# A graph and mixture block on one core: VectorE takes the moments of a later block ahead of the value's bias

## The reference, cut to what matters

```python
def _layernorm(x, axis=-1, eps=1e-05):
    m = jnp.mean(x, axis=axis, keepdims=True)
    v = jnp.var(x, axis=axis, keepdims=True)
    return (x - m) / jnp.sqrt(v + eps)
...
    enh = node_features + 0.1 * query_emb[None, :]
    Q = (enh @ Wq + bq).reshape(N, H, D)
    K = (enh @ Wk + bk).reshape(N, H, D)
    V = (enh @ Wv + bv).reshape(N, H, D)
...
    xn = _layernorm(x, axis=-1)
    x = x + _L0_gnn_ref(xn, edge_index, edge_type_64, ...) + _L0_mix_ref(xn[None], ...)[0]
```

## Time and profile before

| | |
|---|---|
| median of 3 runs | 2975.46 us (2974.98 to 2976.96) |
| profiled execution, its own time | 2994.86 us |
| its span | 2993.0 us |
| busy: TensorE, VectorE, GpSimd, ScalarE | 75%, 64%, 49%, 29% |
| `stage_project` in the span | about 19.6 to 211 us |

### The profile page before, as it was taken

One profiled execution on the slowest core, in us unless ns is written; L12 is line 12 of the kernel. 1 busy time (PEld: TensorE's weight loads), 2 busy tenths in 40 slices (PEclk: granted clock), 3 DMA queues, 4 the chain that ended last, 5 costly groups with the idle time before them and its releaser, 6 DMA issues. The chain is left out here.

```text
span 2993.0 us, 48887 instructions
## 1 busy us (share of the span) xinstructions
PE 2231.8 (75%) x11266; PEld 1389.1 (46%) x11267; DVE 1922.4 (64%) x3248; ACT 868.0 (29%) x2658; POOL 1478.5 (49%) x1460
## 2 busy tenths in 40 slices
PE   6863667666766766766676748999985999967997
PEld 3431333333333333333333436666654666546886
DVE  5653666666666666666666879999995666541111
ACT  2430011011101101100100177777761555531221
POOL 3555555555555555555555226666644434214442
PEclk9995777777777777777777779999997999978999
DMA  4545878787888788878778837777744444354541
GB/s 151 183 156 172 275 257 266 256 270 247 261 270 265 246 264 265 257 249 272 249 253 265 191 129 233 236 235 237 239 150 149 159 146 169 113 192 182 174 169 55
DMA packets 347414, 636.52 MB, mean 213 GB/s; under 512 B 36018, under 2 KB 224950, under 8 KB 347227
## 3 DMA queue, kind: packets, MB, share of 16 engines
q1 hardware_dynamic: 269259, 373.23, 37.9%
q0 software_dynamic: 77824, 262.55, 27.8%
q10 hardware_dynamic: 272, 0.00, 0.0%
HBM read 461.16 MB, written 175.42 MB: 213 GB/s over the span
## 5 line engine op out<-in xcount | busy, mean ns | idle before, releaser
L698 POOL DMA_INDIRECT s_kv<-kv_d,s_index x832 | 795.0, 956 | 657.6 <-issue 325.0
L829 PE MATMUL s_q_ps<-q,s_is_dst 128*128 x2496 | 511.7, 321 | 399.7 <-DVE s_key L752 272.5
L829 PEld LDWEIGHTS s_q_ps<-q,s_is_dst 128*128 128x128 bf16 x2496 | 210.6, 105 | 572.3 <-issue 506.5
L1190 PE MATMUL a_sum_ps<-a_w,a_is_dst 128*128 128x260 f32 x1664 | 421.8, 397 | 48.4 <-DVE odd_sums L1157 31.5
L748 DVE TENSOR_TENSOR s_key<-s_kv,s_rel_ps 128x1024 f32<-128x1024 f32 x208 | 252.4, 1214 | 230.1 <-remote 222.8
L1125 POOL TENSOR_TENSOR a_w<-a_v,a_w 128x512 f32<-128x512 f32 x208 | 284.7, 1369 | 225.2 <-ACT a_w L1095 173.0
L1190 PEld LDWEIGHTS a_sum_ps<-a_w,a_is_dst 128*128 128x128 f32 x1664 | 300.8, 190 | 169.3 <-DVE odd_sums L1157 123.2
L1103 ACT ACTIVATE a_w<-a_v,a_w 128x64 f32<-128x64 f32 x1248 | 319.9, 334 | 3.9 <-DMA a_v<-v_d 3.8
L834 PE MATMUL s_rel_ps<-rel,s_is_kind 64*128 64x64 bf16 x2496 | 244.7, 207 | 52.5 <-issue 51.9
L647 ACT COPY scores<-s_part 128x32 f32 (+1 forms) x104 | 22.6, 218 | 835.9 <-issue 708.6
L757 DVE TENSOR_REDUCE s_part<-s_key 128x16 f32<-128x1024 f32 x208 | 253.7, 1220 | 10.7
(11 more groups left out here) (295 smaller groups left out, 3030.4 us busy)
## 6 DMA issues: line engine op xcount, KB each, us to landing
v_d<-s_kv SPq DMA_DIRECT2D x208, 512.0 KB
a_v<-v_d SPq DMA_DIRECT2D x208, 512.0 KB, 5.3
s_local<-local_d SPq DMA_DIRECT2D x106, 256.0 KB
xh_d<-h_hid SPq DMA_DIRECT2D x24, 1024.0 KB, 6.9
s_kind<-type_d SPq DMA_DIRECT2D x212, 64.0 KB
s_kv<-kv_d,s_index POOLq DMA_INDIRECT x832
kv_d<-pkv SPq DMA_DIRECT2D x50, 256.0 KB, 2.0
wd<-in_L_ffn_Wd SPq DMA_DIRECT2D x8, 1024.0 KB, 12.2
```

Source lines behind the costliest of these rows:

```text
L698: nc.gpsimd.indirect_dma_start(out=kv[:, g * GROUP + b, :], out_offset=None, in_=R["kv"], in_offset=bass.IndirectOffsetOnAxis(ap=index[:, ...
L829: nc.tensor.matmul(q_ps[b][:, u, :], is_dst[:, h, e], M["q3"][:, bass.ds(regs[g % GROUPS * GROUP + u], 1), j, :] .rearrange("p a c -> p (a ...
L1190: ins = nc.tensor.matmul(sum_ps[g % 2 * GROUP + u][:], is_dst[:, g % WRING, u, :], w[:, g % WRING, u, :], start=True, stop=True)
```

## The change

VectorE's addition of the value's bias becomes a function `add_value`, and `normalise` can call it between the aggregation (L262) and the reciprocal (L265). In the loop it is called there, so the order on VectorE becomes: query, key, the three waits, statistics and aggregation of block g + 2, value of block g, reciprocal, normalised block g + 2. The two calls of `normalise` ahead of the loop stay without it. No instruction is added or taken away, and no other engine's program is changed.

```diff
+            def add_value(u, n):
+                dve.wait_ge(S["v_done"], n + 1)
+
+                dve.wait_ge(S["k_read"], n + 1)
+                nc.vector.tensor_tensor(kv[:, u, C:], v_ps[:], bias[:, 2 * C:], ALU.add).then_inc(S["kv_ready"], 1)
+
+            def normalise(st, w, n, value=None):
...
                 nc.vector.bn_aggr(mv[:], stats[:]).then_inc(S["mv_ready"], 1)
+                if value is not None:
+                    add_value(w, value)
 
                 dve.wait_ge(S["std_ready"], n + 1)
                 nc.vector.reciprocal(rstd[:], std[:]).then_inc(S["rstd_ready"], 1)
...
-                    dve.wait_ge(S["v_done"], g + 1)
-
-                    dve.wait_ge(S["k_read"], g + 1)
-                    nc.vector.tensor_tensor(kv[:, u, C:], v_ps[:], bias[:, 2 * C:], ALU.add).then_inc(S["kv_ready"], 1)
-
                     dve.wait_ge(x_in[u], (i + 2) * 16)
                     dve.wait_ge(S["turned"], g + 1)
                     dve.wait_ge(xn_out[u], (i + 1) * 16)
-                    normalise(st, u, g + 2)
+                    normalise(st, u, g + 2, g)
```

More of the change, by code:

```diff
@@ L253, in _ @@
             nc.vector.memset(zero[:], 0.0).then_inc(S["zeroed"], 1)
-            def normalise(st, w, n):
+            def add_value(u, n):
[3 more added lines that the diff above has]
+            def normalise(st, w, n, value=None):
                 dve.wait_ge(S["xn_ready"], n)
```

## The result

The changed kernel takes 3029.41 us in the median of 4 runs (3026.59 to 3032.63), the kernel before 2976.21 us (2974.98 to 2980.85) beside it: 53 us more, a ratio of 1.0177 with a 95% interval of 1.0164 to 1.019.

What follows compares the result with a forecast made beforehand. The prediction took a sync-queue and VectorE chain closed every block as the bound: 0.74 + 0.54 + 2.04 + 0.53 + 0.18 + 0.64 = 4.67 us. 51.0 us over 49 steps plus 1.24 gave 3028 us, range 3012 to 3051.

Steps and rivals of the forecast that it cites:

- The mechanism: In `stage_project`, sync queue and VectorE close a chain every block instead of every two: 4.67 us against 3.63; chance 0.82.
- store to load: In the sync queue, from the store of key and value to the load of x: 0.91 or 0.57, mean 0.74 us.
- store to statistics: From the normalised block's store being issued to VectorE's statistics starting: 2.04 us, with a median landing of 2.0.
- aggregation to bias: On VectorE, from aggregation to the value's bias: 0.18 us, taken between a lower bound of 0.10 and an upper of 0.28.
- The head and the tail: At `stage_project`'s ends: first bias unmoved at 30.4, a late next store adding 1.24 us, last store equally far behind its bias.
- The wait's total: VectorE's statistics waiting every block for the normalised block's store: 85 to 100 us in all instead of 7.1.
- What the change buys: On VectorE, the bias fills the 0.36 us deviation wait and the 0.52 us value wait goes; both worth nothing.
- The rival on the other side: The change pays: with a store landed within 0.57 us, TensorE sets 3.2 us a block, 2954 us; chance 0.04.
- The clock: Rival: TensorE, busy 65%, falls to a lower clock in `stage_project`; 3094 us or part of it; chance 0.07.
- The DMA's price: Landing time of the stage's DMAs: median kept; the shortest, 1.8 us, would give 4.43 us a block and 3016.
- The part absorbed: Rival: the sync queue gets ahead somewhere, so half the loss remains, 3001 us; chance 0.05.
- no change: Rival: waits for value and store trade places in `stage_project`, pace stays 3.63 us, total 2975 us; chance 0.02.

Runs made afterwards that it cites:

- run 1: Kernel before with only the value's bias moved behind the wait for the normalised block's store, still ahead of the statistics: 3007.02 us against 2988.91, ratio 1.0054.
- run 2: Changed kernel with VectorE's wait for the normalised block's store moved right ahead of the instruction writing that buffer: 3020.21 us against 2988.91 for the kernel before.
- run 5: Changed kernel plus one 128 x 256 VectorE addition a block behind the key, in the time spent waiting for the store: 2655.67 us, ratio 1.0201 to the kernel before.
- run 6: Changed kernel plus one 128 x 256 VectorE addition a block between the aggregation and the value's bias: 2670.47 us, ratio 1.0261 to the kernel before.
- run 3: Changed kernel with the store of key and value issued from ScalarE's queue: 2964.69 us, ratio 0.9918 to the kernel before.
- run 7: Changed kernel with the store of key and value put behind the next block's load and normalised-block store in the sync queue: 2577.56 us, ratio 0.9904 to kernel before.
- run 10: Repeat, in the last group, of the changed kernel with key and value stored behind the next block's load and normalised-block store: 2577.60 us, ratio 0.9899 to kernel before.
- run 8: The changed kernel again, unaltered, on another chip: 2654.85 us, ratio 1.0201 to the kernel before.

## Why the prediction was right

**The mechanism** held: the statistics wait for `xn_d` in every block, the pace is set by the chain of queue and VectorE, and runs 1, 2, 5 and 6 each move the pace by what they move in this chain, run 1 within 0.04 us. Runs 3 and 7 cut it without touching VectorE's order, and the loss goes.

**The terms** of the sum, by the timeline of the changed kernel: store to load 0.74 (foreseen 0.74) and load to store 0.54 (0.54), as means over all blocks; store to statistics 2.13 over 49 blocks (2.04), between 1.93 and 3.03; statistics to aggregation 0.53 (0.53); aggregation to bias 0.10 (0.18), the lower of the two bounds; bias to the issue of its store 0.63 (0.64). Unrounded, the sum is 4.68 where 4.67 was foreseen, by two errors of 0.09 and 0.08 that offset each other. Over 49 steps they would have made 4 us either way.

**The head and the tail.** The loop from the first to the last bias takes 229.3 us, against 177.7 before: 51.6 us more; foreseen were 51.0 + 1.24. The first step is 5.42 us instead of the foreseen 5.9. The first bias, which was to stay at 30.4, came at 29.4; this 1.0 us lies between the 51.6 and the 50.7 of the stage's row. In the traces of the other runs it starts at 29.3 to 30.6, so nothing is read into it.

**The regularity** was wrong: steps of 4.50 and 4.84 in turn were foreseen, and the timeline shows 4.61 and 4.72 in the mean of 24 steps each. The queue's shorter turn is followed by the longer way from the store to the statistics: behind 0.58 us 2.27 (153.15 to 155.42), behind 0.91 us 2.03 (158.14 to 160.17), and 2.23 and 2.00 in the mean over all blocks but the first ones. The mean isn't affected, and why the landing answers to it isn't shown.

**The wait's total** was foreseen at 85 to 100 us and is 108.3. The single wait is 2.21 us in the mean of 49, from 2.08 to 2.43, in the upper part of the foreseen 1.7 to 2.3 and in eight blocks above it; and 49 waits of 1.7 to 2.3 would make 83 to 113 us, so the total was also given too narrowly. In every second block the query and the key end 1.08 us behind the issue of the store of key and value (152.04 to 153.12), in the others after the foreseen 1.3. This has no part in the pace.

**What the change buys.** That it was worth nothing while VectorE waits for the store was right. The rival on the other side priced it, without that wait, at 21 us less than the kernel before. Runs 3, 7 and 10 found 24 to 27 us less, at a pace of 3.07 to 3.08 instead of 3.2. Its condition was made true by another way, a queue in which nothing urgent waits for the bias, and not by a faster landing.

**The clock** didn't fall. TensorE is busy for 147.00 of 226 us, 65%, and the granted clock is 1.00 throughout; the rival drew its case from the scores stage, with the same share and 0.74. It was nearer than that looks: with 0.3 us more idle time a block it fell in run 6. That a fallen clock here and there would fit into the block, as the prediction argued, run 6 bears out; up to 10 us had been allowed for it in the range, and nothing was lost. **The DMA's price**: the Trainium skill's sentence in "DMA: Bandwidth & Descriptors", "Latency and other measured facts", that lighter load makes the fixed cost smaller, agrees in direction only. From 100 to 125 the stage moves 136 GB/s instead of 174, and the median landing of the store is 1.9 us instead of 2.0; the time from its issue to the statistics was no shorter for it, 2.13 in the mean against 1.94 and 2.04.

**The part absorbed** and **no change** are out by the pace in every block.

## What to carry to other kernels

Before an instruction is moved behind a wait, ask what its own signal releases, and follow the queue that it releases to the end: if the thing waited for stands in it further down, in program order, the wait feeds itself, and the latency of a DMA is paid in every round. A small wait for a DMA that shows up every second block, like the 7.1 us here, is the sign that such a chain is already near. An order that loses for this reason may be a good one: putting the slow member of the queue behind the urgent ones made a gain of 1% out of a loss of 1.8%.

## What the runs showed of the hardware that was not expected

The mean busy share doesn't tell TensorE's clock. In the changed kernel it is busy for 65% of 226 us, in bursts of 3 us with idle stretches of 1.65 in the mean and at most 2.1, and stays at the upper of its two levels. In the scores stage of the kernel before it is busy for 65.58 of 100 us, with idle stretches up to 7.5 us, and alternates between the two levels, with a mean of 0.74. In run 6, with the same bursts and idle stretches of 1.95 in the mean and at most 2.3, it alternates too, with a mean of 0.91: one more instruction on VectorE, 0.3 us a block, was enough to bring TensorE's clock down. It did so in each of its four executions, whose mean over the whole program is 0.881 to 0.885, against 0.889 to 0.892 in those of runs 5 and 8.

An instruction's duration isn't what it adds to a chain: the additional 128 x 256 addition is listed with 0.39 us in run 6 and moved the next instruction by 0.31. In run 5 the same addition is listed with 0.64 us in the median and cost nothing at all.

The chips differ in one part of the program. For the same program, the changed kernel, the stretch 600 to 700 in the scores stage reads on the chip of the result and on that of run 8:

```profile
600.00:700.00 100.00, 68.68 (x400) 36.50 (x400) 67.42 (x79) 9.52 (x33) 54.17 (x57) 0.76 0.81 265
```

```profile
600.00:700.00 100.00, 86.94 (x560) 48.10 (x560) 92.59 (x110) 14.59 (x50) 75.91 (x80) 0.83 1.03 359
```

The second does 560 matmuls where the first does 400, at 359 GB/s instead of 265, and the whole span is 2652.7 instead of 3029.6 us. The tiles and scores stages and the rest behind them, on the chip of run 8:

```profile
262.00:1376.00 1114.00, 906.75 (x5850) 500.51 (x5849) 993.25 (x1184) 152.28 (x520) 800.99 (x840) 0.81 1.00 339
1376.00:2652.70 1276.70, 1076.55 (x4906) 781.86 (x4906) 800.87 (x1680) 639.04 (x1934) 565.92 (x407) 0.94 0.52 175
```

The first takes 1114 us instead of 1491, which is the whole difference; the second agrees within 0.1 us, and `stage_project` runs at 4.67 and 4.68 us a block. What differs between the chips was not looked into.
